# Audio tower, one core: another order of the queues in the attention front, and the folded bias joined by one VectorE instruction

## What is computed

```python
h = tok(x, W, b)                                   # patches @ W.T + b
h = h + attn(layernorm(h), Wq, Wk, Wv, Wo)
h = h + ffn(layernorm(h), w_gate_up, w_down)       # silu(gate) * up, then down
# in attn, per series and head, with 10 queries i and 10 keys j:
scores = rope(q) @ rope(k).T / sqrt(32), causal
tmp = softmax(scores); heavy = argmax_j(sum_i tmp)             # heavy budget: 1 key
probs = softmax(where(heavy | abs(i - j) <= 1, scores, neg))   # "band": |i - j| <= 1
out = (probs @ v) @ Wo.T
```

## Time and profile before

| | us |
|---|---|
| median of 3 runs | 288.92 (288.78 to 289.41) |
| the profiled execution | 288.86 |
| its span, first to last instruction | 286.9 |
| PE busy | 274.6 (96%) |
| DVE busy | 160.8 (56%) |
| ACT busy | 80.3 (28%) |
| POOL busy | 54.7 (19%) |

### The profile page before, as it was taken

The page is one execution under the profiler, slowest core; times in us unless marked ns, Lnnn a source line. Parts: engine busy times, 40 slices in busy tenths (PEclk is TensorE's granted clock), DMA queues, the critical chain, the costliest instruction groups (busy, mean ns, idle before and its releaser), DMA issues.

```text
span 286.9 us, 4588 instructions
## 1 busy us (share of the span) xinstructions
PE 274.6 (96%) x1781; PEld 215.9 (75%) x1781; DVE 160.8 (56%) x309; ACT 80.3 (28%) x151; POOL 54.7 (19%) x44
## 2 busy tenths in 40 slices
PE   7979999998899999999999999999999999999994
PEld 6455477664586877776876666799999999999993
DVE  2582987779669998696904435463333334333323
ACT  2211123431321001423011103263434444343320
POOL 0123000001006150003600000133222222332210
PEclk9999999999999999999999999999999999999999
DMA  7992130000002524353412033286334433330003
GB/s 226 425 404 82 43 112 0 5 2 0 1 2 110 163 102 177 116 193 130 144 77 73 37 112 111 110 271 243 110 111 146 148 142 110 110 110 0 0 0 110
DMA packets 6816, 32.76 MB, mean 114 GB/s; under 512 B 977, under 2 KB 977, under 8 KB 6289
## 3 DMA queue, kind: packets, MB, share of 16 engines
q1 hardware_dynamic: 6512, 32.15, 32.0%
q10 hardware_dynamic: 288, 0.39, 0.4%
HBM read 31.23 MB, written 1.31 MB: 113 GB/s over the span
## 4 chain that ended last, share of the span: by engine, by line
PE 91%; DVE 4%; ACT 1%; issue 1%; POOL 0%; DVEq 0%
PE ps L210 35%; PE ps L1076 20%; PE ps L1086 10%; PE ps L1013 6%; PE ps L951 4%; PE ps L1005 4%; PE ps L966 3%; PE ps L929 2%; PE ps L956 2%; PE ps L882 2%; PE ps L1018 1%; DVE prod L238 1%; PE ps L993 1%; PE ps L935 1%; DVE stats L553 1%
## 5 line engine op out<-in xcount | busy, mean ns | idle before, releaser
L210 PE MATMUL ps<-xT,wgu 128*128 128x384 f32 x384 | 70.9, 340 | 0.1
L210 PEld LDWEIGHTS ps<-xT,wgu 128*128 128x128 f32 x384 | 68.1, 188 | 2.5 <-DVE xT L584 0.9
L1076 PE MATMUL ps<-whole,stage 128*128 128x256 f32 (+1 forms) x288 | 58.3, 357 | 1.4 <-ACT whole L369 1.4
L1076 PEld LDWEIGHTS ps<-whole,stage 128*128 128x128 f32 x288 | 49.6, 190 | 12.2 <-issue 4.8
L789 DVE TENSOR_TENSOR gu<-silu,ps 128x256 f32<-128x256 f32 (+1 forms) x32 | 15.5, 484 | 67.6 <-PE ps L210 44.7
L303 POOL TENSOR_TENSOR wd<-stage,wd 128x512 fp32r<-128x512 f32 x16 | 26.9, 1681 | 78.6 <-ACT wd L369 78.6
L210 PE MATMUL ps<-wd,hT 128*128 128x512 f32 x144 | 35.6, 393 | 0.0
L474 ACT ACTIVATE silu<-ps 128x256 f32<-128x256 f32 (+1 forms) x32 | 14.0, 438 | 75.1 <-PE ps L1076 48.6
L210 PEld LDWEIGHTS ps<-wd,hT 128*128 128x128 f32 x144 | 26.8, 188 | 5.0
L1086 PE MATMUL ps<-stage,gu 128*128 128x512 f32 x64 | 30.1, 592 | 0.0
L369 ACT ACTIVATE wgu<-stage 128x1024 fp32r<-128x1024 f32 x16 | 16.9, 1058 | 22.7 <-PE ps L210 20.9
(11 more groups left out here) (101 smaller groups left out, 250.5 us busy)
## 6 DMA issues: line engine op xcount, KB each, us to landing
stage<-w_ffn SPq DMA_DIRECT2D x32, 768.0 KB, 4.3
stage<-w_k SPq DMA_DIRECT2D x1, 1024.0 KB, 6.7
stage<-w_q SPq DMA_DIRECT2D x1, 1024.0 KB, 10.1
stage<-w_v SPq DMA_DIRECT2D x1, 1024.0 KB, 12.2
wo<-w_o SPq DMA_DIRECT2D x1, 1024.0 KB, 13.9
out<-ob SPq DMA_DIRECT2D x14, 64.0 KB, 2.4
const<-consts SPq DMA_DIRECT2D x1, 800.0 KB, 8.1
out<-ob ACTq DMA_DIRECT2D x6, 64.0 KB, 1.9
```

Source lines behind the costliest of these rows:

```text
L210: ins = pe.matmul(dst, lhs[a], rhs[b], start=first and n == 0, stop=last and n == 2)
L1076: ins = pe.matmul(ps[:, bank, at + a:at + b], stage[:, slot, w:w + P], xf[:, k, a:b], start=k == 0, stop=k == KT - 1)
```

## The change

Five things are changed, all in the front:

1. The bias. ACT no longer writes `fold_less`, and POOL's `bias_sum` is gone. A new function on DVE, `bias_join`, computes `fold_bias = fold_hi * sign + fold_part` in one instruction (the signs are a column of the constants). It is called three times on DVE: behind `token_scale(1)`, behind `rotate("k", 2)` and behind `early_products(9)`.
2. PE's start. The first two k projections stand ahead of `spread_scale(0)`, and wait for ACT to have read the first fold's bias.
3. ACT's queue. `exponential(0)` stands between the two `chunk_out`, and exponentials 2 and 3 behind the first three drains where they stood behind all nine.
4. DVE's queue. `softmax_out(0)` stands ahead of `place(1)`, and all eight value products ahead of `softmax_out(3)`.
5. PE's end of the front. Both `value_sums` stand ahead of both `project_out`, and `spread_scale(1)` behind the transposes of tile 1.

```diff
-            def bias_sum(x):
-                pool.wait_ge(fold_bias_parts, x + 1)
-                pool.tensor_tensor(fold_bias[:, x], fold_part[:, x], fold_less[:, x], ALU.add).then_inc(fold_bias_set, 1)
...
-            bias_sum(0)
             key_add(0)
             key_add(1)
             key_add(2)
-            bias_sum(1)
-            bias_sum(2)
...
                 act.activation(fold_part[:, x], bank, ACT.Copy, scale=cut["low"]).then_inc(fold_bias_read, 1)
-                act.wait_ge(fold_bias_hi, x + 1)
-                act.activation(fold_less[:, x], f32(fold_hi[:, x]), ACT.Copy, scale=cut["sign"]).then_inc(fold_bias_parts, 1)
...
             chunk_out(0)
+            exponential(0)
             chunk_out(1)
-            for n in range(2):
-                exponential(n)
-            for item in DRAIN[:9]:
+            exponential(1)
+            for item in DRAIN[:3]:
                 drain(item)
-            for n in range(2, 4):
-                exponential(n)
+            exponential(2)
+            exponential(3)
+            for item in DRAIN[3:9]:
+                drain(item)
...
+            def bias_join(x):
+                dve.wait_ge(fold_bias_hi, x + 1)
+                dve.wait_ge(fold_bias_read, x + 1)
+                dve.scalar_tensor_tensor(fold_bias[:, x], f32(fold_hi[:, x]), cut["sign"], fold_part[:, x], ALU.mult, ALU.add)\
+                   .then_inc(fold_bias_set, 1)
...
             token_scale(1)
+            bias_join(0)
             token_scale(2)
...
             rotate("k", 2)
+            bias_join(1)
             rotate("q", 0)
...
             early_products(9)
+            bias_join(2)
             place(0)
             softmax_in(0)
             dve.wait_ge(product_set, NPOS)
             step(score_reduce(9))
+            softmax_out(0)
             place(1)
             softmax_in(1)
-            softmax_out(0)
             softmax_out(1)
             heavy_keys()
             softmax_in(2)
             softmax_in(3)
             softmax_out(2)
-            values(0, 7, 6)
+            values(0, 7, 6, 5, 4, 3, 2, 1, 0)
             softmax_out(3)
-            values(0, 5, 4, 3, 2, 1, 0)
...
             fold_weight(0)
+            project(("k", 0, 0), ("fold bias", 0))
+            project(("k", 0, 1), ("fold bias", 0))
             pe.wait_ge(apart_set, 3)
             read_out("embedding", 1)
             spread_scale(0)
-            for n in range(3):
-                project(("k", 0, n), ("embedding", 0))
+            project(("k", 0, 2), ("embedding", 0))
...
             value_sums(0, ("projection", ("q", 1, 0)))
+            value_sums(1, ("projection", ("k", 1, 2)))
             project_out(1, 1, ("projection", ("k", 1, 1)))
-            value_sums(1, ("projection", ("k", 1, 2)))
             project_out(0, 2, ("projection", ("q", 1, 2)))
-            read_out("projection", ("q", 1, 1))
-            pe.wait_ge(apart_set, NT)
-            spread_scale(1)
...
             transposes(LN2[1], ("wo", 1))
+            read_out("projection", ("q", 1, 1))
+            pe.wait_ge(apart_set, NT)
+            spread_scale(1)
             pe.wait_ge(xf_sb, 1)
             gate_up_whole(0, 1)
```

More of the change, by code:

```diff
@@ L149, in audio_tower @@
         fold_hi, fold_bias = (sb(n, [P, 3, DH], F32R, early_mem) for n in ("fold_hi", "fold_bias"))
-        fold_part, fold_less = (sb(n, [P, 3, DH], F32, early_mem) for n in ("fold_part", "fold_less"))
+        fold_part = sb("fold_part", [P, 3, DH], F32, early_mem)
         quarter = sb("quarter", [P, P], F32R, early_mem)
@@ L184, in audio_tower @@
         apart_set, scale_mm, scale_sb = sem("apart_set"), sem("scale_mm"), sem("scale_sb")
-        fold_mm, fold_sb, fold_bias_mm, fold_bias_hi, fold_bias_read, fold_bias_parts, fold_bias_set = (
-            sem(n) for n in ("fold_mm", "fold_sb", "fold_bias_mm", "fold_bias_hi", "fold_bias_read", "fold_bias_parts", "fold_bias_set"))
+        fold_mm, fold_sb, fold_bias_mm, fold_bias_hi, fold_bias_read, fold_bias_set = (
+            sem(n) for n in ("fold_mm", "fold_sb", "fold_bias_mm", "fold_bias_hi", "fold_bias_read", "fold_bias_set"))
         product_set, chunk_mm, chunk_sb, place_mm, placed = (
```

## The result

| | before | after |
|---|---|---|
| median, us | 289.01 (288.78 to 289.41, 4 runs) | 284.85 (284.14 to 285.02, 4 runs) |
| ratio | | 0.985, 95% interval 0.983 to 0.987 |
| profiled execution, us | 288.86 | 284.75 |
| its span, us | 286.9 | 282.8 |

Faster by 1.5%. The forecast was 284.9 with a range of 284.2 to 286.3.

The account below looks back on a forecast made before the run. PE's queue was taken as the bound, so only its pauses before 82.17 us could go: 1.69 in the front plus 3.05 around the output projections, less 0.75 given back, 4.0 us; 288.9 to 284.9, range 284.2 to 286.3.

Parts of the forecast that it names:

- part 1: PE's start: two k projections ahead of the scale matmul, which then no longer waits for its input; 1.10 us gained.
- part 2: Bias joined on DVE instead of ACT and POOL: PE's pause at the second bias falls from 0.70 to 0.11; 0.59 us gained.
- given back ahead of tile 0: Before tile 0's transposes: DVE's tables, then layer norm, come later, so PE waits 0.7 us; some 0.75 of 4.74 lost.
- Part 3: Exponentials and softmax earlier on ACT and DVE: PE never waits for a value product again; 0.55 us gained.
- Part 4: Both value sums ahead of the output projections: two waits of 0.73 us gone, and 0.23 us less per projection.
- Part 5: Tile 1's transposes ahead of the scale matmul: first gate matmuls at 72.38 against 77.12, with 0.3 us of new wait.
- A: Rival: DVE's join is held up by POOL's last key addition, total 285.6 us; chance 0.09.
- B: Rival: DVE's softmax comes forward no more than 1.69 us, second value sums end at 65.0, total 285.9 us; chance 0.06.
- C: Rival: PE's wait for tile 0 doesn't appear because DVE works faster, total 284.1 us; chance 0.05.
- D: As a rival: the gain is given back in the first pass, where DVE doesn't follow PE, about 288.9 us; chance 0.03.
- E: Rival: ACT's six drains behind exponential 3 stop PE's last v projection, slower than before, 289.8 us; chance 0.03.

Follow-up runs that it names:

- the experiment with the scale matmul: The changed kernel with spread_scale(1) back ahead of the transposes of tile 1: 283.96 us against 288.81 before, ratio 0.9817.
- part 2 alone: The kernel before with only the bias joined on DVE, scale matmul still ahead of all k projections: 289.05 us, ratio 1.0015.
- part 3 alone: The kernel before with only exponentials ahead of drains, softmax_out(0) ahead of place(1), value products ahead of softmax_out(3): 287.77 us against 288.81, ratio 0.9964.
- parts 4 and 5 alone: The kernel before with only both value sums ahead of both output projections and spread_scale(1) behind tile 1's transposes: 288.1 us against 288.81, ratio 0.9965.
- part 1 alone: The kernel before with only two k projections ahead of the scale matmul: 287.66 us against 289.02, ratio 0.9938.

## Why the prediction was right

The forecast's 4.0 us were 3.65 inside the span. In D, step by step:

| place | forecast earlier by | measured |
|---|---|---|
| part 1, two k projections first | 1.10 | 1.26 (alone) |
| part 2, join | 0.59 | 0.40 (on top of part 1) |
| q projection's bias matmul | 1.69 | 1.66 (D 11.93 to 10.27) |
| first value sums | 1.69 | 1.78 (46.38 to 44.60) |
| first gate matmuls | 4.74 | 4.51 (61.74 to 57.23) |
| given back ahead of tile 0 | 0.75 | 0.83 |
| from gate 2 to the end | 4.0 | 3.68 and 3.65 |

**Parts 1 and 2.** The sum held, its two terms were off against each other. In part 1 I had kept the 4.16 us that the scale matmul took with its projections; in its new place, with its input long ready, the stretch takes 3.97 (15.42 to 19.39 in the chain). In part 2 I had 0.04 us from ACT's end to the join, 0.29 for the join and 0.05 to hand over; they are 0.11, 0.35 and 0.14, so PE's wait was 0.33 and not 0.11. The gain of 0.40 is 0.19 short of the 0.59, inside the 0.1 to 0.2 that I had allowed for the join's length, though more than half of it came from the handovers.

**Part 3.** The clock times stand almost as told, once the 0.62 us of earlier start are added to those of after. The heavy-key part was put at 47.5 and starts at 46.90 + 0.62 = 47.52. The products start at 54.34 + 0.62 = 54.96 (55.1). `softmax_out(0)` fits ahead of `place(1)`. Only the share was told too small: the prediction credits part 3 with the wait of 0.55 us alone, and it was worth 1.02 to 1.16. The rest isn't missing from the sum, where it stands among the 0.54 us by which 36 transposes in a row are shorter.

**Part 4.** PE has no pause from the first value sum to the end of the projections, and the stretch is 10.96 us (10.83).

**Part 5.** The mechanism was right: the wait appeared where it was put, 0.70 us (0.7), and it was caused as said, which the experiment with the scale matmul shows. The term that was mis-sized is the transposes. I had charged what they took in the chain of before, where PE came straight from other work:

```profile
75.94 0.51 PE ps L993 x4
...
80.96 0.54 PE ps L993 x4
```

In the chain of after, behind a pause:

```profile
70.65 0.67 PE ps L994 x4
...
76.53 0.67 PE ps L994 x4
```

0.16 and 0.13 us more. In part 4 I had counted 0.23 us per projection as the price of a start from a pause, and should have charged the same where my own sum made two new pauses. That is most of the 0.35 us that the forecast was too high.

**The total.** That 284.85 came so near to 284.9 is luck. Inside the span the forecast was 0.35 too high; the rest came from outside the sum: in the profiled execution of after the start was 0.62 us shorter and what follows DVE's last addition 0.17 longer, which with the 3.65 gives the 4.1 us between the two spans. A later set of the same kernel gave a median of 285.37. Both lie inside the range.

**The rivals.** A, the join behind POOL's key addition: POOL's additions run from 21.09 for 3.23 us, so to 24.32, and the join's start at 24.54 is 0.11 us behind ACT's end (24.07 + 0.36 = 24.43). With part 2 alone POOL's additions were over at 23.45 (20.13 + 3.32), and the join at 26.06 stood 0.10 us behind ACT's end (25.60 + 0.36): the same distance with POOL out of the way. So the join was not held up after, though only 0.22 us lie between POOL's end and its start. The first pass shows the same blocking as before (`by_cos` 2.78 us at 83.12 beside POOL's products from 82.94), but no run here puts it on the join. B fell (the products are done at 59.78, before PE asks for the last of them at 63). C fell, the wait came. D fell: D from gate 2 to the end is 200.10 us after (263.21 - 63.11) and 200.07 before. E fell: the k and q drains ran from 53.14 to 56.2 and PE never waited for one, not even with part 3 alone.

## What to carry to other kernels

When an instruction is moved behind another to take it off the critical engine, look at who waits for it and what stands behind that on the other queue: here 0.3 us were hidden on PE and 0.9 lost through DVE, and the old place would have been free, since the new order had a wait there that it could have filled. A small instruction pays only in the order that gives it cover: the same join was worth 0.4 us behind one move and nothing that could be told without it. And price each new pause with the slower start that comes with it, and each pause taken away with more than the trace writes down as a wait.

## What the runs showed of the hardware that I had not expected

**In some executions the granted clock falls, and only in kernels that still have the long pause at the start.** The profiled execution of parts 4 and 5 alone still has the pause of 1.73 us ahead of the scale matmul. The stretch from 17.90 to 20.50 us (busy us of PE, PEld, DVE, ACT, POOL with counts, granted clock, DMA share, GB/s), and the timeline:

```profile
17.90:20.50 2.60, 2.60 (x35) 1.67 (x34) 1.11 (x4) 0.00 (x0) 0.00 (x0) 0.50 1.01 418
```

```profile
17.59 0.39 PE L984 MATMUL ps<-apart,const 128*128 128x12 f32 x2 [1.73 <-DVE apart L578]
17.91 1.94 PE L951 MATMUL ps<-fold,pat 128*32 128x128 f32 x32
19.77 0.80 PE L956 MATMUL ps<-fold_bias,quarter 128*128 128x512 f32 x1
```

The clock granted is 0.50, the level of 1.2 GHz, and the 32 matmuls take 1.94 us that take 1.06 to 1.08 in every other profile. By D the q projection's bias matmul comes 1.47 us late (13.40 against 11.93). It is the only one of the fourteen profiles in which the clock falls before PE's work is over. All executions of the experiments list a mean clock. Sorted by whether the kernel's trace has the pause:

| kernels | executions | with a mean clock of 0.994 or less | their times |
|---|---|---|---|
| before (three sets), part 3 alone, parts 4 and 5 alone, part 2 alone: pause of 1.7 to 2.0 us | 95 | 32 | before: 289.6 to 291.3, where its other 38 executions take 287.9 to 289.4 |
| all with the k projections first: pause of 0.66 us or none | 61 | 0 | |

A third of the executions of one sort, and none of the other. No mean lies between 0.994 and 0.996, and the means of 0.996 to 0.999 come from elsewhere: in the other thirteen profiles the clock falls only once PE is done (after: 0.68 in the stretch from 282.0 to 282.5 us, 0.50 from there on), which costs nothing. So part 1 did something besides its 1.26 us: with it went a pause behind which the clock fell now and then, at a price of some 2 us each time (for before the medians are 290.5 and 288.6). The prediction had settled the clock by one profile of before, where it stayed at 1.00.

Apart from the four executions of the changed kernel in the result, both sorts of kernels were run in the same sets on the same chips. But only one profile shows the fall in its place, and the two sorts differ in the order of PE's queue there and not in the pause alone, so the pause as the cause is likely and not shown; why it takes only a third of the executions no run here tells either. It also means that medians of before in the experiments hold such executions: in the set of 289.02 and 285.37 the executions of before without a fallen clock have a median of 288.62, and the gain over them is 3.25 us, where the two medians give 3.65 and the first set 4.16. The 3.65 of D are free of it.

**The start scatters.** The first folded bias ends between 14.76 and 16.14 us in the fourteen profiles with nothing changed ahead of it. The two latest are part 1 alone (16.13) and the scale matmul back (16.14). In both the matmuls with `dims` start at 8.39 us, right behind the landing of a load, as with part 1 alone:

```profile
8.39 1.35 PE L922 MATMUL ps<-dims,average 128*128 128x160 f32 x8 [1.51 <-DMA dims<-w_dims]
```

The load of `w_dims` took 4.4 us from issue to landing after, 4.7 before and 6.1 in these two, of the same bytes issued at the same time (2.28 or 2.29 us). This 1.4 us of scatter is more than most parts of the change are worth, which is why the distances D tell more here than medians of six runs.
